# Softmax weights: TensorE transposes through PSUM replaced by an fp16 split in SBUF and a DMA transpose

## The reference

```python
x = x + attn(layernorm(x))        # 32 query heads of 128, 8 key/value heads, causal
x = x + fake_quant(layernorm(x)) @ fake_quant(ctx)      # ctx: 2 x 1024 x 1024
x = x + ffn(layernorm(x))         # 64 experts of rank 8, the 16 best gated by a softmax
```

```python
scores = einsum('bhqd,bhkd->bhqk', q, k) * scale
scores = where(causal, scores, -1e9)
attn = softmax(scores, axis=-1)
out = einsum('bhqk,bhkd->bhqd', attn, v)
out = out.transpose(0, 2, 1, 3).reshape(b, s, H * D) @ Wo.T
```

## Time and profile before

| | |
|---|---|
| median of 3 runs | 1232.4 us |
| span of the profiled execution | 1233.0 us |
| TensorE matmul busy | 1195.8 us (97%), 7088 matmuls |
| DVE busy | 797.5 us (65%) |
| ACT busy | 476.1 us (39%) |
| POOL busy | 224.6 us (18%) |
| line 1213 (transposes of the weights) | 640 matmuls, 91.0 us |
| DMA | 67.78 MB, mean 55 GB/s |

### The profile page before, as it was taken

One profiled execution on the slowest core, in us unless ns is written; L12 is line 12 of the kernel. 1 busy time (PEld: TensorE's weight loads), 2 busy tenths in 40 slices (PEclk: granted clock), 3 DMA queues, 4 the chain that ended last, 5 costly groups with the idle time before them and its releaser, 6 DMA issues.

```text
span 1233.0 us, 20119 instructions
## 1 busy us (share of the span) xinstructions
PE 1195.8 (97%) x7088; PEld 664.7 (54%) x7088; DVE 797.5 (65%) x1782; ACT 476.1 (39%) x1082; POOL 224.6 (18%) x310
## 2 busy tenths in 40 slices
PE   5999999999999999999999999999999999979997
PEld 4865555555555555555555555555555554445553
DVE  8747665666566656765666566656665667789873
ACT  4446630663066306620563056305630563122211
POOL 3003310330034002410231023102320231000000
PEclk9999999999999999999999999999999999989999
DMA  6102202112011201120012002200220034000001
GB/s 250 68 3 69 94 30 92 66 38 94 1 53 49 94 0 43 59 94 0 33 69 94 0 20 82 94 0 12 90 94 0 8 114 153 1 1 18 35 35 52
DMA packets 21484, 67.78 MB, mean 55 GB/s; under 512 B 2368, under 2 KB 2496, under 8 KB 21440
## 3 DMA queue, kind: packets, MB, share of 16 engines
q1 hardware_dynamic: 21440, 67.19, 15.4%
HBM read 58.80 MB, written 8.39 MB: 54 GB/s over the span
## 4 chain that ended last, share of the span: by engine, by line
PE 84%; DVE 10%; ACT 3%; issue 1%; DMA 0%; POOL 0%; DVEq 0%; ACTq 0%
PE ps L1100 74%; PE ps L1213 5%; PE ps L1339 3%; ACT prob L620 1%; DVE prob L894 1%; DVE stats L737 1%; DVE q_t L729 1%; DVE prob_t L729 1%; ACT q_t L498 1%; PE ps L1355 1%; DVE prob L753 1%; PE ps L1406 1%; DVE wq_sb L729 1%; DVE o_t L729 0%; DVE wo_sb L729 0%
## 5 line engine op out<-in xcount | busy, mean ns | idle before, releaser
L1100 PE MATMUL ps<-h_t,wq_sb 128*128 128x512 f16 x1536 | 350.6, 379 | 0.0
L1100 PE MATMUL ps<-wo_sb,o_t 128*128 128x512 f16 x1536 | 342.4, 379 | 7.3 <-DVE x_sb L866 2.3
L475 POOL TENSOR_SCALAR prob<-prob,row_inv 128x128 f32<-128x128 f32 (+3 forms) x256 | 184.3, 738 | 761.8 <-DVE row_inv L854 761.8
L620 ACT ACTIVATE prob<-prob,neg_max 128x128 f32<-128x128 f32 (+3 forms) x256 | 140.5, 549 | 314.8 <-DVE neg_max L900 314.8
L866 DVE SCALAR_TENSOR_TENSOR x_sb<-ps,x_sb 128x512 f32<-128x512 f32 x256 | 176.0, 691 | 132.7 <-PE ps L1100 132.7
L1100 PEld LDWEIGHTS ps<-wo_sb,o_t 128*128 128x128 f16 x1536 | 147.7, 98 | 191.3 <-DVE q_t L729 9.4
L1100 PEld LDWEIGHTS ps<-h_t,wq_sb 128*128 128x128 f16 x1536 | 150.3, 98 | 155.6
L729 DVE SCALAR_TENSOR_TENSOR o_t<-ps,o_t 128x512 f16<-128x512 f32 x64 | 44.2, 691 | 149.4 <-ACT o_t L498 149.4
L498 ACT ACTIVATE prob_t<-ps 128x512 f16<-128x512 f32 (+1 forms) x192 | 92.6, 517 | 120.6 <-PE ps L1213 120.6
L1100 PE MATMUL ps<-prob_t,v_sb 128*128 128x512 f16 (+3 forms) x768 | 114.8, 299 | 0.0
L1100 PE MATMUL ps<-k_t,q_t 128*128 128x384 f16 (+3 forms) x768 | 114.8, 299 | 0.0
(11 more groups left out here) (113 smaller groups left out, 968.1 us busy)
## 6 DMA issues: line engine op xcount, KB each, us to landing
wq_in<-in_wq SPq DMA_DIRECT2D x32, 512.0 KB, 6.1
wo_in<-in_wo SPq DMA_DIRECT2D x32, 512.0 KB, 4.3
side_in<-in_ctx SPq DMA_DIRECT2D x16, 512.0 KB, 4.2
x_sb<-in_x SPq DMA_DIRECT2D x8, 512.0 KB, 8.7
ctx_quantised<-side_out SPq DMA_DIRECT2D x16, 256.0 KB, 2.1
h_t<-ctx_quantised SPq DMA_DIRECT2D x2, 2048.0 KB, 8.9
out<-x_sb SPq DMA_DIRECT2D x8, 512.0 KB, 2.6
o_t<-in_wdown SPq DMA_DIRECT2D x4, 512.0 KB, 7.9
```

The costliest lines, as they stand in the source:

```text
L475: ins = nc.gpsimd.tensor_scalar(at, at, row_inv[:, u % 2, q:q + 1], S_P, ALU.mult, ALU.mult)
L620: ins = nc.scalar.activation(at, at, ACT.Exp, bias=neg_max[:, n % 2, q:q + 1], scale=SOFTMAX, accum_out=row_sum[:, n % 2, q:q + 1])
L1100: ins = nc.tensor.matmul(out_, lhs(i), rhs(j), start=start and n == 0, stop=stop and n == 3 * len(pairs) - 1)
```

## The change

For each unit ACT and DVE now split the normalised `prob` straight from SBUF, all 1,280 columns at once, into the high and low rows of a new buffer `prob_s` (float16, one buffer, not two). SP then issues one `dma_start_transpose` that writes both parts, 20 blocks of 128x128, into `prob_t`, and raises `p_turned`. TensorE's `turn` is gone. ACT's split of unit n stands at the head of step n + 1, ahead of that step's exponentials, and waits for the landing of unit n - 1, since `prob_s` has one buffer. The outputs of unit n wait for `p_turned`. A unit's blocks now lie by query tile, so `outputs` reads `prob_t` with a stride of four blocks and does tile 0 with a product of its own (15 matmuls of the same 3,840 columns in place of 12); the order of the query tiles in PSUM and in `o_t` changes with it. SP's lists are written anew around the transposes.

```diff
-S_AT = {2: 0, 0: 3 * P, 3: 4 * P, 1: 8 * P}
-S_BANKS = ((2, 0), (3,), (1,))
+S_AT = {3: 0, 2: 4 * P, 0: 7 * P, 1: 8 * P}
+S_BANKS = ((3,), (2, 0), (1,))
...
+        prob_s = sb("prob_s", [P, 2, S_COLS], F16)
+        prob_t = sb("prob_t", [P, 2, 2, S_BLOCKS, P], F16)
...
+            def turn(g, n):
+                sp.wait_ge(p_lo, UNITS * g + n + 1)
+                sp.sem_inc(sp_passed)
+                if not (isinstance(g, int) and g == 0 and n < 2):
+                    sp.wait_ge(pv_done, UNITS * g + n - 1)
+                    sp.sem_inc(sp_passed)
+                sp.dma_start_transpose(prob_t[:, n % 2, :, :, :].rearrange("p a b n -> p (a b) n"),
+                                       prob_s[:, :, :].rearrange("p a n -> p (a n)")).then_inc(p_turned[n % 2], 16)
...
             def first_group():
+                turn(0, 0)
+                load_wq((0, 4))
+                load_up(0)
+                turn(0, 1)
                 load_side(0, True, 1, b_w[:, 1, :])
+                load_wo((0, 2))
+                turn(0, 2)
                 load_side(0, True, 2, b_w[:, 2, :])
+                load_wq((0, 5))
+                turn(0, 3)
                 load_side(0, True, 3, b_w[:, 3, :])
+                load_wo((0, 3))
+                turn(0, 4)
                 load_side(0, True, BT, ctx_in[0])
+                load_wq((0, 6))
+                turn(0, 5)
+                load_wo((0, 4))
+                turn(0, 6)
...
+                load_side(1, False, 0, ctx_in[2])
...
             def group(g, last):
+                turn(g, 0)
+                if last:
+                    load_a(0)
+                else:
+                    load_wq((g, 4))
+                    load_up(g)
+                turn(g, 1)
+                load_wo((g, 2))
+                turn(g, 2)
                 store_ctx(g, False, 0)
                 load_side(g, False, 1, ctx_in[2 * g + 1])
...
+            for n in range(2):
+                sp.dma_start(wo_in[:, n, :], wo[n]).then_inc(wo_loaded[n], 16)
+            load_side(0, True, 0, b_w[:, 0, :])
+            for n in range(2, 4):
+                load_wq((0, n))
...
+                def p_split(n):
+                    act.wait_ge(prob_normed, UNITS * g + n + 1)
+                    if not (first and n == 0):
+                        if n >= 1:
+                            act.wait_ge(p_turned[(n - 1) % 2], 16 * (UNITS // 2 * g + (n - 1) // 2 + 1))
+                        else:
+                            act.wait_ge(p_turned[1], 16 * (UNITS // 2 * g))
+                    split_hi(prob_s[:, 0, :], prob[:, n % 2, :], p_hi, 1.0)
...
+                    if 1 <= u <= UNITS:
+                        p_split(u - 1)
                     if u < UNITS and not short:
                         exponentials(u)
...
+                def p_split(n):
+                    dve.wait_ge(p_hi, UNITS * g + n + 1)
+                    split_lo(prob_s[:, 1, :], prob[:, n % 2, :], prob_s[:, 0, :], p_lo, 1.0)
...
-                def turn(n, i):
...
                 def outputs(n):
-                    pe.wait_ge(pt_lo, 3 * (UNITS * g + n) + 2)
+                    pe.wait_ge(p_turned[n % 2], 16 * (UNITS // 2 * g + n // 2 + 1))
...
+                    split_product(ps[:, PV_BANK, O_AT[0]:O_AT[0] + P],
+                                  [(lambda i: v_sb[:, i, n % 2, 0, :], lambda j: prob_t[:, n % 2, j, S_AT[0] // P, :])])
+                    for k in range(QT):
+                        tiles = QT - max(k, 1)
+                        ins = split_product(ps[:, PV_BANK, 0:tiles * P],
                                             [(lambda i: v_sb[:, i, n % 2, k, :],
+                                              lambda j: prob_t[:, n % 2, j, k:k + 4 * tiles - 3:4, :])],
+                                            start=k == 0, stop=k == QT - 1)
...
+    nc = bacc.Bacc("TRN2", target_bir_lowering=False, num_devices=1, dynamic_dma_scratch_size=1024)
```

More of the change, by code:

```diff
@@ L45 @@
 MASKED = -1.0e30
-S_AT = {2: 0, 0: 3 * P, 3: 4 * P, 1: 8 * P}
-S_BANKS = ((2, 0), (3,), (1,))
[L50 to L54, removed]
+S_AT = {3: 0, 2: 4 * P, 0: 7 * P, 1: 8 * P}
+S_BANKS = ((3,), (2, 0), (1,))
+S_BLOCKS = 10
+S_COLS = S_BLOCKS * P
+O_AT = {q: (QT - 1 - q) * P for q in range(QT)}
 PV_BANK = 5
@@ L295, in decoder_layer @@
         scores_done = sem("scores_done")
-        pt_done = sem("pt_done")
+        p_turned = [sem(f"p_turned{n}") for n in range(2)]
         pv_done = sem("pv_done")
@@ L410, in group @@
                 if last:
-                    load_a(0)
-                    load_wo((g, 2))
                     load_a(1)
-                    load_wo((g, 3))
+                else:
+                    load_wq((g, 5))
+                turn(g, 3)
+                load_wo((g, 3))
+                turn(g, 4)
+                if last:
                     load_a(2)
+                else:
+                    load_wq((g, 6))
+                turn(g, 5)
+                if last:
                     load_a(3)
                     load_ctx(0)
-                    store_ctx(g, False, 1)
+                else:
+                    load_wo((g, 4))
+                turn(g, 6)
+                store_ctx(g, False, 1)
+                if not last:
+                    load_side(g + 1, False, 0, ctx_in[2 * g + 2])
+                    load_wq((g, 7))
+                turn(g, 7)
+                if last:
                     load_ctx(1)
                 else:
[L421 to L426, removed]
+                    load_wo((g, 5))
+            for n in range(2):
[3 more added lines that the diff above has]
+                load_wq((0, n))
             first_group()
@@ L1199, in wo_chunk @@
                     t, half = c // 2, c % 2
+                    at = t // QT * SEQ + O_AT[t % QT]
                     split_product(ps[:, bank, :],
-                                  [(lambda i, n=n: o_t[:, n, i, t * P:(t + 1) * P],
+                                  [(lambda i, n=n: o_t[:, n, i, at:at + P],
                                     lambda j, n=n: wo_sb[:, n, j, half * HALF:(half + 1) * HALF])
                                    for n in (2 * pair, 2 * pair + 1)]).then_inc(gen_done, 1)
-                def turn(n, i):
-                    if not (first and n == 0 and i < 2):
-                        pe.wait_ge(pt_lo, 3 * (UNITS * g + n) + (0, -1, 1)[i])
-                    at = 0
-                    for k in PT_TURNS[i]:
-                        for q in range(k, QT):
-                            ins = nc.tensor.transpose(
-                                ps[:, PT_BANK[i], at:at + P],
-                                prob[:, n % 2, S_AT[q] + k * P:S_AT[q] + (k + 1) * P], ident[:, :])
-                            at += P
-                    ins.then_inc(pt_done, 1)
                 def outputs(n):
-                    pe.wait_ge(pt_lo, 3 * (UNITS * g + n) + 2)
+                    pe.wait_ge(p_turned[n % 2], 16 * (UNITS // 2 * g + n // 2 + 1))
                     if n == 0 and not first:
```

75 lines of the change are left out of this document (17 added, 58 removed).

## The result

The changed kernel takes 1203.27 us (median of 4 runs, 1200.88 to 1205.26) against 1232.45 us for the kernel before on the same chip (1232.38 to 1234.06): ratio 0.9761, interval 0.9747 to 0.9775. It is faster by 29 us where 11 were forecast: sign and range held, the size did not. The profiled span is 1201.3 us, 31.7 us less than before.

What follows compares the result with a forecast made beforehand. TensorE's queue, busy 97%, was taken as the bound. Removing 70 us of transposes and adding waits summed to 40X - 255, or -11 us at X = 6.1: 1221 us from a median of 1232.4, range 1170 to 1350.

Steps and rivals of the forecast that it cites:

- TensorE's step: Middle step of an attention group: 9.53 us less 1.09 us for its 10 transposes, so 8.44 us.
- The hops around the chain: ACT's split 1.27, DVE's split 1.50 and 0.3 us of waits and hops: 3.1 us a unit besides X.
- X: Time of the 640 KB transposing DMA from issue to landing, taken as 6.1 us; 5.4 to 6.7 in the forecast.
- hidden rival: Transposing DMA mostly covered, X of 3.3 to 5.3, few waits left, 1180 us at 4.5; chance 0.20.
- Both signs: Prediction wrong if X is outside 5.4 to 6.7, or if TensorE waits for prob_s's chain in steps 7 to 9.
- The fine source rows: The transposing move is cut into 256-byte source rows, so 6.1 us was taken, not the low end.
- the low end: Low bound of X: 640 KB as plain traffic, judged from stores out of SBUF, would take 2.9 us.
- my row: The wq load, 512 KB in 6.1 us, nearest in size to the transposing move and taken for X.
- The late side loads: Group 0: loads of b_w parts 1 to 3 and ctx 0 behind the transpose; four steps of X + 6.4 instead of 10.17.
- none from step 7: TensorE's waits for prob_s's chain end there; from step 6 steps of 13.6 us cover X up to 10.5.
- The break-even: Whole kernel: X = 6.4 us, where the 70 us saved are nearly all given back; slower from there on.
- The 70 us taken off TensorE: Attention groups: 10 transposes of 64 units removed, 64 x 1.09 = 70 us, credited in full to TensorE.

Runs made afterwards that it cites:

- side_first: The changed kernel, but in group 0 SP issues each side load or store ahead of that step's transpose; 1188.45 us, ratio 0.964 to the kernel before.
- longer_turn: side_first with 10 further blocks per unit transposed ahead of the 20, into a buffer nobody reads; 1240.51 us, ratio 1.006 to the kernel before.
- before_fewer_turns: The kernel before with 3 of 10 transposes a unit in groups 1 to 7, part of the computation left out; 1223.03 us, ratio 0.9918.
- two_dmas: side_first with two transposing DMAs of 10 blocks a unit, high part after ACT's split, low part after DVE's; 1171.36 us, ratio 0.9495.
- high_part_only: side_first with only the high part transposed, 10 blocks in one DMA, and read twice, part of the computation left out; 1171.0 us, ratio 0.9494.
- exp_ahead_of_split: side_first, but ACT takes the next unit's exponentials before it splits prob_s; 1327.0 us, ratio 1.0759 to the kernel before.

## Why the prediction was right or wrong

**TensorE's step: right.** 8.44 us was worked out and 8.44 measured; ACT's split 1.27 and 1.27, DVE's 1.50 and 1.49; outputs of 15 matmuls with strided reads 1.69 us instead of 1.63, 4 us in all (64 x 0.06) of the 0 to 21 us that I had bounded them by. The hops around the chain were right as well: ACT 357.96 to the next issue 360.93 is 2.97 us, 3.1 were taken.

**X: the term that was mis-sized.** This is the step that failed first: 6.1 was taken from the nearest load by size, 4.9 measured, below the forecast's 5.4 to 6.7 and in the hidden rival's 3.3 to 5.3. Both signs by which the prediction called itself wrong came: X outside its bounds, and waits in steps 7 and 8 (of group 7, below). By the prediction's own conditions at X = 4.9 a group would wait 1.6 us in step 2 and nothing in steps 3 to 6: -7.1 us; the measured groups have -6.3, with 1.84 and 0.54 us of waits. The fine source rows, which I held against the low end, are there, but cost little: the packets under 512 bytes went from 2,368 to 168,256, and the wq load beside them lands in 4.2 us, not slower than before. The estimate from the Trainium skill ("DMA: Bandwidth & Descriptors", section "Latency and other measured facts"), X near 4.5, came nearer than my row. 10 more blocks, 327,680 bytes, took 4.9 - 3.4 = 1.5 us here, some 218 GB/s (an estimate from the two landings) where that section states 261 for a non-contiguous middle dimension. The 1309 ns a block of the Trainium skill's "VectorE: DVE Perf Modes", section "The three transpose paths", is not borne out for blocks in one DMA: 4.9 / 20 = 0.245 us.

**Group 0: the place was right, the price was not.** The late side loads were predicted, at a loop of X + 6.4 = 11.3 us for X = 4.9; it took 13.8 to 14.2 in three steps of four. DVE's split of b_w (1.2 us, in the earlier trace rows) and the maxima of the next scores (some 1.8 us) stand in DVE's queue ahead of the split of prob_s, and I left both out of the loop, where I had ACT's 1.27; and the load landed 8.05 us after the transpose's start, not X + 2.3 = 7.2, since its issue stood 3.17 us behind. The lower clock added 4.1 us. At X = 4.9 my terms give +1.7 us for the group, it was +10.7. side_first shows what the queue's order costs: with the loads ahead group 0 takes 123.7 us instead of 137.95.

**Group 7: overlooked.** Its last steps have no products for a next group, so they are shorter and cover less. TensorE waits 1.35, 1.39 and 1.46 us in its steps 6, 7 and 8, where I had written "none from step 7", and the group has -4.2 us instead of -7.1. The last of them, from the timeline of weight loads:

```profile
1003.24 1.64 PEld L1133 LDWEIGHTS ps<-prob_t,v_sb 128*128 128x128 f16 x15 [1.46 <-DMA prob_t<-prob_s]
```

**The sum.** At X = 4.9 the terms give 7 x -7.1 + 1.7 = -48 us. Group 0 lacks 9.0 of that, groups 1 to 6 0.8 each, group 7 2.9: -31.3, against -31.7 between the two profiles (-29 by the medians). So X alone does not explain the miss: with the right X these terms overshoot to -48. That sign and range held owes something to luck, since a transfer taken too slow stood beside a group 0 and a group 7 taken too cheap.

**The break-even.** X = 6.4 as the point where the change turns slower was too high: longer_turn has X = 6.4, a mended group 0, and is slower at 1.006. I had written that a wait costs what it lasts; behind some of the longer waits the clock fell as well, and no term of mine stood for that (11.7 us in groups 1 to 6 of longer_turn; without them it would take some 1229 us, an estimate from these two numbers).

**The 70 us taken off TensorE.** I credited the transposes to TensorE as if nothing stood behind it. before_fewer_turns shows that in the kernel before DVE stood close behind (its steps are still 9.05 to 9.66 us, against 9.53): of 43 us only 9.4 came. The changed kernel's step did shrink by the whole 1.09 us, so the rest of the change freed TensorE of DVE as well, by its new order on DVE, by doing without the PSUM banks between the two, or both; which of them is open. My working saw neither.

## What to carry to other kernels

When work is moved from the bounding engine to a chain through a DMA queue, write down for each step the chain's every link in queue order, including what else stands in the queue of each engine that it passes; the first and the last group, with other neighbours and less cover, cost more here against the sum (9.0 and 2.9 us) than the six in the middle together (4.8). Check what the next engine's order would allow before crediting the work removed. And split the transfer where the data come in two parts: here the first half then cost nothing, and only the second was in the chain (two_dmas took as long as high_part_only).

## What the runs showed of the hardware

- The transposing DMA from SBUF to SBUF holds the issuing queue: 3.06 us for 20 blocks of 128x128 fp16, 1.34 for 10, against 0.33 to 0.57 for a plain DMA; it lands 1.8 to 2.1 us after the issue's end. What stands behind it in the queue starts that much later.
- TensorE's granted clock behind waits for prob_t in attention: up to 2.2 us, the outputs and the query product always took their 6.6 us. Between 2.4 and 3.5 us both happened: full speed behind 2.46, 2.77, 2.85, 3.22, 3.49 and 3.50 us, the 1.2 GHz level for some microseconds behind 2.51, 2.57 and 3.37 to 3.44. Behind all waits of exp_ahead_of_split from 3.56 us up, and behind 4.83 and 6.55 us in the changed kernel, it came back at the lower level, and the two pieces took 7.9 to 9.6 us. What decides between 2.4 and 3.5 us, these runs do not show.
